# Attention in pairs of heads, in two row halves of TensorE, with fp32r parts in place of bf16 parts

## The reference

```python
q = (x @ Wqa @ Wqb).reshape(b, s, H, D)
kv = (x @ Wkva @ Wkvb).reshape(b, s, KVH, D, 2)
k, v = (kv[..., 0], kv[..., 1])
q = _rope(q)
k = _rope(k)
scores = jnp.einsum('bqhd,bkhd->bhqk', q, k) * scale
scores = jnp.where(causal[None, None], -jnp.inf, scores)
w = jax.nn.softmax(scores, axis=-1)
out = jnp.einsum('bhqk,bkhd->bqhd', w, v).reshape(b, s, E)
return out @ Wout + bout
```

## Time and profile before

| | us |
|---|---|
| median of 3 runs | 2591.58 |
| lowest, highest | 2581.57, 2600.53 |
| span of the profiled execution (first to last instruction) | 2609.7 |
| latents and routing | 0 to 199.4 |
| attention | 199.4 to 1299 |
| mixing | 1710 to 1859 |

### The profile page before, as it was taken

The page is one execution under the profiler, slowest core; times in us unless marked ns, Lnnn a source line. Parts: engine busy times, 40 slices in busy tenths (PEclk is TensorE's granted clock), DMA queues, the critical chain, the costliest instruction groups (busy, mean ns, idle before and its releaser), DMA issues. The chain is left out here.

```text
span 2609.7 us, 44812 instructions
## 1 busy us (share of the span) xinstructions
PE 2234.0 (86%) x12898; PEld 1283.6 (49%) x12898; DVE 1772.8 (68%) x3458; ACT 1179.7 (45%) x2552; POOL 772.4 (30%) x613
## 2 busy tenths in 40 slices
PE   5866889999999999999879999967578887798777
PEld 2322333333333333333369999946345544454446
DVE  3656667778887778777433333346498889988892
ACT  1222556666666666666644454411123333343332
POOL 3333333000000000000023333355156666566651
PEclk9756989999999999999989999976689898898897
DMA  7423333111111111111142223156400000000004
GB/s 280 130 70 104 96 104 103 57 56 58 58 58 56 58 56 58 57 57 57 30 146 94 97 81 109 49 159 196 145 1 16 17 17 0 16 16 16 9 0 141
DMA packets 140179, 191.32 MB, mean 73 GB/s; under 512 B 19256, under 2 KB 116416, under 8 KB 137920
## 3 DMA queue, kind: packets, MB, share of 16 engines
q1 hardware_dynamic: 111392, 139.92, 16.6%
q0 software_dynamic: 9120, 31.47, 3.7%
q10 hardware_dynamic: 19584, 18.88, 2.1%
HBM read 125.34 MB, written 60.29 MB: 71 GB/s over the span
## 5 line engine op out<-in xcount | busy, mean ns | idle before, releaser
L912 DVE TENSOR_REDUCE at_piece_max<-at_A 128x1 f32<-128x512 f32 (+3 forms) x1280 | 740.9, 605 | 249.3 <-PE at_A L809 205.9
L778 ACT ACTIVATE at_wt<-at_B 128x512 f32<-128x512 f32 (+3 forms) x1280 | 607.9, 537 | 339.1 <-PE at_B L833 211.9
L806 PE MATMUL at_A<-at_ka,at_qa 96*128 96x512 bf16 (+3 forms) x1280 | 459.1, 361 | 79.2 <-DMA at_ka<-k_parts 76.2
L830 PE MATMUL at_B<-at_qb,at_kb 99*128 99x512 bf16 (+3 forms) x1280 | 446.2, 353 | 1.7 <-ACT at_wt L778 0.6
L850 PE MATMUL at_O<-at_wt,at_v 128*32 128x512 f32 (+3 forms) x2496 | 339.2, 548 | 0.4 <-ACT at_wt L778 0.4
L806 PEld LDWEIGHTS at_A<-at_ka,at_qa 96*128 96x128 bf16 x1280 | 126.2, 99 | 432.7 <-DVE at_piece_max L912 245.8
L1176 POOL TENSOR_TENSOR s_down<-lw_down_full,s_down 128x256 fp32r<-128x256 f32 x10 | 7.3, 729 | 873.9 <-ACT lw_down_full L1168 873.9
L1353 PE MATMUL ex_H<-ex_xT,ex_w_in 128*128 128x256 f32 x1920 | 247.5, 285 | 3.2 <-DVE ex_xT L1460 3.2
L1353 PEld LDWEIGHTS ex_H<-ex_xT,ex_w_in 128*128 128x128 f32 x1920 | 236.6, 192 | 3.6 <-DVE ex_w_out L1465 3.6
L2051 POOL TENSOR_TENSOR l_sumy<-l_sumy,l_scaled 128x1024 f32<-128x1024 f32 x72 | 220.1, 3057 | 27.9 <-ACT l_scaled L2201 26.6
L2251 DVE TENSOR_TENSOR l_order<-l_order 128x1024 f32<-128x1024 f32 x112 | 221.2, 1975 | 1.9
(11 more groups left out here) (246 smaller groups left out, 3191.2 us busy)
## 6 DMA issues: line engine op xcount, KB each, us to landing
buf<-zeros POOLq DMA_DIRECT2D x10, 1024.0 KB, 20.6
ex_x<-buf SPq DMA_DIRECT2D x40, 256.0 KB, 2.7
expert_out<-ex_y ACTq DMA_DIRECT2D x40, 256.0 KB, 2.2
at_v<-v SPq DMA_DIRECT2D x32, 256.0 KB
ex_raw_in<-in_W_in SPq DMA_DIRECT2D x8, 1024.0 KB, 4.9
q_parts<-parts SPq DMA_DIRECT2D x16, 384.0 KB, 4.5
at_qa<-q_parts SPq DMA_DIRECT2D x32, 192.0 KB
at_ka<-k_parts SPq DMA_DIRECT2D x32, 192.0 KB
```

The source lines that it names most:

```text
L778: act.activation(wt[p % NE_][:, q0:CH], pB_of(p, u)[:, q0:CH], ACT.Exp, scale=D ** -0.5).then_inc(wt_ready, 1)
L806: ins = pe.matmul(pA[b][:, 0:w], qa[u][:, i * P:(i + 1) * P], ka[u][:, k0:k0 + w], start=True, stop=not diag)
L830: ins = pe.matmul(pB_of(p, u)[:, q0:CH], kb[u][:, kt * P:(kt + 1) * P], qb[u][:, j * CH + q0:(j + 1) * CH], start=True, stop=not diag)
L912: dve.tensor_reduce(piece_max[:, i, k0 // CH:k0 // CH + 1], pA[a_step(p) % NA][:, 0:w], AX.X, ALU.max).then_inc(a_used, 1)
```

## The change

In **latents** each of q and k is cut into two fp32r parts instead of three bf16 parts: one ScalarE cast and one GpSimd subtraction, whose result is the second part. The ScalarE casts L274 and the VectorE subtractions L401 are gone. The parts are stored as float32.

In **attention** a round is for a pair of heads that share their k and v. There are 16 rounds of 40 steps, and a step has two A pieces and two B pieces. The two heads stand in rows 0 to 63 and 64 to 127 of the operands, with three groups of 16 rows each (high by high, high by low, low by high) and, for B, two more rows for the maxima. Each pair of pieces waits once, for both buffers it needs; NA and NB stay 3, and NE_ is 16. The mask matmuls are gone: VectorE takes the diagonal maxima with a tensor_tensor_reduce that adds the mask from SBUF, and GpSimd zeroes the hidden half of each diagonal 128 x 128 block of wt by an affine_select. `values` handles four key tiles for both heads, eight matmuls in the four column groups (two groups a head, even and odd key tiles). The turn is four float32 matmuls with a 0/1 matrix of 64 columns that adds the two groups of each head, and ScalarE's `keep` copies result and sum to attn undivided. The loads are 12 two-dimensional DMAs of 16 rows for each of load_a and load_b, with one more for v, and four DMAs put rows of ones into kb before the first piece. GpSimd's indirect DMAs are tied to the rounds, two token tiles in each.

In **mixing** VectorE inverts the sums of all tiles at the start (512 in each partition), and GpSimd, behind its four gathers of a tile, writes at[u] as the product of attn and these; SyncE's copy is gone.

```diff
-PARTS = 3
+PARTS = 2
 VW = 32
 
-RUNS = ((0, 3), (3, 2), (5, 1))
-STACK = 6 * D
+Q_TERMS, K_TERMS = (0, 0, 1), (0, 1, 0)
+STACK = len(Q_TERMS) * D
+HP = 2
+BASE = P // HP
+HPAIRS = B * H // HP
...
-                pool.tensor_tensor(rest[k][0:rows], rot[k][0:rows], parts[k][0:rows, 0],
-                                   ALU.subtract).then_inc(rest_ready, 1)
+                pool.tensor_tensor(parts[k][0:rows, 1], rot[k][0:rows], parts[k][0:rows, 0].bitcast(F32),
+                                   ALU.subtract).then_inc(low_ready, 1)
...
-            def mid(c, k):
-                act.wait_ge(rest_ready, PAIRS * c + k + 1)
-                act.copy(parts[k][0:rows_of(k), 1], rest[k][0:rows_of(k)]).then_inc(mid_ready, 1)
...
-            def low(c, k):
-                dve.wait_ge(mid_ready, PAIRS * c + k + 1)
-                dve.tensor_tensor(parts[k][0:rows_of(k), 2], rest[k][0:rows_of(k)], parts[k][0:rows_of(k), 1],
-                                  ALU.subtract).then_inc(low_ready, 1)
...
-        NA, NB, NE_ = 3, 3, 8
+        NA, NB, NE_ = 3, 3, 16
         MR = PARTS
-        qa = [sb(f"qa{u}", [STACK, S], BF16) for u in range(2)]
-        ka = [sb(f"ka{u}", [STACK, S], BF16) for u in range(2)]
-        qb = [sb(f"qb{u}", [STACK + MR, S], BF16) for u in range(2)]
-        kb = [sb(f"kb{u}", [STACK + MR, S], BF16) for u in range(2)]
+        HALF_T = QT // 2
+        QKS = STACK + MR
+        qa = [sb(f"qa{u}", [P, S], F32R) for u in range(2)]
+        ka = [sb(f"ka{u}", [P, S], F32R) for u in range(2)]
+        qb = [sb(f"qb{u}", [P, S], F32R) for u in range(2)]
+        kb = [sb(f"kb{u}", [P, S], F32R) for u in range(2)]
...
+        def a_slot(p, h):
+            return HP * p + h + 2 * (p > M1_AT) + 2 * (p > M0_AT)
...
+        def stack(q, k, n):
+            for h in range(HP):
+                for r in range(len(Q_TERMS)):
+                    rows = slice(BASE * h + r * D, BASE * h + (r + 1) * D)
+                    cols = bass.ds(n // (H // HP) * S, S)
+                    yield q[rows, :].bitcast(F32), d["q_parts"][Q_TERMS[r], bass.ds(n % (H // HP) * HP * D + h * D, D), cols]
+                    yield k[rows, :].bitcast(F32), d["k_parts"][K_TERMS[r], bass.ds(n % (H // HP) // 2 * D, D), cols]
...
+            sp.wait_ge(ones_made, 1)
+            for u in range(2):
+                for h in range(HP):
+                    rows = kb[u][BASE * h + STACK:BASE * h + QKS, :]
+                    sp.dma_start(rows.rearrange("a (j n) -> a j n", n=CH).bitcast(F32),
+                                 ones[:].bitcast(F32).unsqueeze(1).to_broadcast([MR, NQ, CH])).then_inc(ones_in, 16)
...
+            def causal(n, p, h):
+
+                j, kt, q0 = Bp[p]
+                N = PER_B * n + HP * p + h
+                block_ = wt[(HP * p + h) % NE_][:, q0:q0 + P]
+                pool.wait_ge(wt_ready, N + 1)
+                pool.affine_select(block_, block_, [[1, P]], ALU.is_ge, 0.0, base=0,
+                                   channel_multiplier=-1).then_inc(hidden, 1)
+
+            fetch(0)
+            for n in range(HPAIRS):
+                for p in range(NPC):
+                    if p == END[1]:
+                        dispatch(n)
+                    if p == END[2] and n + 1 < HPAIRS:
+                        fetch(n + 1)
+                    if Bp[p][1] >= 4 * Bp[p][0]:
+                        for h in range(HP):
+                            causal(n, p, h)
...
+            def keep(n, j):
+                G = NQ * n + j
+                act.wait_ge(oT_made, G + 1)
+                dst = attn[:, bass.ds(n // (H // HP) * QT + j * TPC, TPC), bass.ds(n % (H // HP) * HP, HP), :]
+                src = pX_of(j).rearrange("p t (h n) -> p t h n", h=HP)[:, :, :, 0:D + 1]
+                act.copy(dst, src).then_inc(o_kept, 1)
...
+            def pieces_a(n, u, p):
                 i, k0, w = A[p]
-                N = PER_A * n + a_step(p)
-                b = a_step(p) % NA
                 if p == 0:
-                    pe.wait_ge(a_in[u], 6 * 16 * (n // 2 + 1))
+                    pe.wait_ge(a_in[u], LOADS * (n // 2 + 1))
+                wait(pe, a_used, PER_A * n + a_slot(p, HP - 1) - NA + 1)
+                for h in range(HP):
+                    rows = slice(BASE * h, BASE * h + STACK)
+                    pe.matmul(pA[a_slot(p, h) % NA][:, 0:w], qa[u][rows, i * P:(i + 1) * P], ka[u][rows, k0:k0 + w],
+                              start=True, stop=True).then_inc(a_made, 1)
...
+                wait(pe, wt_ready, PER_B * n + HP * p + 1 - NB + 1 + (u == 0 and p == 0))
+                for h in range(HP):
+                    rows = slice(BASE * h, BASE * h + QKS)
+                    pe.matmul(pB_of(p, h, u)[:, q0:CH], kb[u][rows, kt * P:(kt + 1) * P],
+                              qb[u][rows, j * CH + q0:(j + 1) * CH], start=True, stop=True).then_inc(b_made, 1)
...
             def values(n, u, p4):
+                pe.wait_ge(wt_ready, PER_B * n + HP * (p4 + VG))
+                wait(pe, hidden, PER_D * n + DIAG[p4 + VG])
+                j = Bp[p4][0]
+                if Bp[p4][1] == 0:
+                    wait(pe, o_kept, NQ * n + j - 1)
+                for p in range(p4, p4 + VG):
+                    kt, q0 = Bp[p][1:]
+                    for h in range(HP):
+                        rows = slice(VW * (2 * h + kt % 2), VW * (2 * h + kt % 2 + 1))
+                        late = kt == 1 and q0 > 0
+                        if late:
+                            pe.matmul(pO[j % 2][rows, 0:q0], blank[:], wt[(HP * p4 + h) % NE_][:, 0:q0],
+                                      start=True, stop=False)
+                        pe.matmul(pO[j % 2][rows, q0:CH], vs[u][:, kt // TPC, kt % TPC, :],
+                                  wt[(HP * p + h) % NE_][:, q0:CH], start=kt < 2 and not late,
+                                  stop=kt >= 4 * j + 2).then_inc(wt_used, 1)
...
-                    ins = pe.transpose(pX_of(j)[:, t, :], raw[j % 2][:, t * P:(t + 1) * P], ident[:])
+                    ins = pe.matmul(pX_of(j)[:, t, :], raw[j % 2][:, t * P:(t + 1) * P], summing[:], start=True, stop=True)
...
+                    p4 = p - LAG - VG + 1
+                    if p4 % VG == 0:
+                        if p4 >= 0:
+                            values(n, u, p4)
                         elif not first:
-                            values(n - 1, 1 - u, NPC - 3 - LAG + p)
+                            values(n - 1, 1 - u, NPC + p4)
...
+                        if p == (END[j] + LAG + VG - 1) % NPC and not (late and first):
+                            turn(n - late, j)
...
+                if diagonal:
+                    ins = dve.tensor_tensor_reduce(junk[(HP * i + h) % 4][:, 0:w], pA[slot % NA][:, 0:w], hide[:, CH - w:CH], 1.0, NEG,
+                                                   ALU.add, ALU.max, accum_out=top)
+                else:
+                    ins = dve.tensor_reduce(top, pA[slot % NA][:, 0:w], AX.X, ALU.max)
+                ins.then_inc(a_used, 1)
...
+                wait(pool, aT_made, t - 1)
+                both = bass.ds(2 * t, 2)
+                pool.tensor_tensor(at[u][:].rearrange("p w (h n) -> p w h n", n=D), s["attn"][:, both, :, 0:D],
+                                   over_sum[:, both].unsqueeze(3).to_broadcast([P, 2, H, D]),
+                                   ALU.mult).then_inc(at_ready, 1)
...
+            pool.wait_ge(sums_inverse, 1)
             rounds(pool, tile)
...
-                sp.dma_start(at[u][:], s["attn"][:, bass.ds(2 * t, 2), :]).then_inc(x_in[u], 16)
...
-                pe.wait_ge(x_in[u], 32 * (t // 2 + 1))
+                pe.wait_ge(at_ready, t + 1)
...
+            dve.reciprocal(over_sum[:], s["attn"][:, :, :, D]).then_inc(sums_inverse, 1)
```

More of the change, by code:

```diff
@@ L834, in piece_b @@
[L834 to L852 removed]
+                    pe.wait_ge(max_in[1], 32 * (n + 1))
@@ L1005, in layer1_weights @@
+            for n in range(HPAIRS):
+                round_(n, n + 1 < HPAIRS)
 def layer1_weights(nc, d, s):
```

412 lines of the change are left out of this document (169 added, 243 removed).

## The result

The change made the kernel slower: 2942.48 us (median of 4 runs, 2930.61 to 2956.77) against 2591.89 (4 runs), a ratio of 1.135 with a 95% interval of 1.131 to 1.140. The forecast was 2684, the range 2500 to 2790: the sign was right, the size was not, and the time lies outside the range. The profiled execution has a span of 2940.9 us against 2609.7, so 331 us are to be found.

A forecast was written before the change was run, and what follows sets the result against it. The prediction took PE and VectorE to hold each other through three buffers in attention. Attention +80.5 us, mixing +12 and latents 0 made +92.5, so 2684 us on the median, range 2500 to 2790.

The forecast's parts named there:

- The clock: Attention rounds: a quarter of the groups run at 1.2 GHz, adding 5.5 us a round, 64.2 to 69.7; called the weakest term.
- 86 with all: Attention: a round of two heads takes 86 us if all groups run at 1.2 GHz.
- What the clock rests on: PE in attention: fewer rows a us than now but longer bursts; clock near 0.88 on average.
- Rival 1: Attention: PE's clock stays at 2.4 GHz, rounds 64.2 us, +9 us, total 2601 us; chance 0.17.
- The round at 2.4 GHz: Attention, a pair of heads: VectorE work 46.0, idle 16.3, narrow pieces 0.9, correction 1.0, together 64.2 us.
- Rival 2: Attention: full values burst takes 1.0 us, rounds 56.4, total 2476 us; chance 0.29 including values between it and the high-clock rival.
- Rival 3: Attention: row halves do not overlap or selects are late, 2735 us and up; low clock throughout, 2930 us; chance 0.14.
- Latents: Latents stage: casts and third parts go, stored bytes rise by 4/3; 0 us (-5 to +6).
- Fill: Attention's start: first matmul at 225 us against 214.55 before, as twelve small loads replace a few wide ones.
- First pass: Attention's first pass, 80 pieces of A: 48 us, ending at 273 us.
- Last round: Attention's last round, only B: about 60 us, 61 with the clock.
- Mixing: Mixing: reciprocal 3.4 us with hand-overs +5, tiles 0.5 us further apart +7; in all +12 us (+5 to +22).

The follow-up runs named there:

- b1: Changed kernel with A and B matmuls reading all 64 rows of their half, zeros in the unused rows: 2887 us against the changed kernel's 2942, clock 0.79.
- e3: Kernel before without its mask matmuls, A and B reading 64 rows instead of 96 and 99: 2737 us, clock 0.84.
- b2: Kernel before with A matmuls reading 48 of their 96 rows: 2735 us, clock 1.00.
- e2: Kernel before without its 32 mask matmuls a head: 2606 us, clock 0.97.
- d2: Changed kernel with a wait for each single piece instead of one for each couple: 2887 us against the changed kernel's 2942, rounds 80.0 us.
- c1: Changed kernel with A and B reading all 64 rows of their half and each couple of A matmuls issued twice: 2956 us, clock 0.88.

## Why the prediction was wrong

- *The clock* is the step that failed: "I take a quarter of the groups at 1.2: 10 x 0.25 x 2.3 = 5.5" (the product is 5.75). The kind was right and named as the weakest term; both factors were low. At a mean of 0.70 PE spends 60% of the time, about half of the groups, at the low level. And a slow full group costs more than 2.3: the burst 3.64 instead of 1.92, four steps of 1.57 instead of 1.28, together 2.9, with turns of 1.97 instead of 1.10. 83.0 - 67 = 16 us a round instead of 5.5. What had been a bound "86 with all" would be about 100, by the same prices.
- *What the clock rests on*: I set fewer rows against longer bursts and took the middle. A head's matmuls of A and B read 48 and 50 rows where they read 96 and 99, at the same columns, and b1 and e3 show that the rows count; b2 shows that they do not decide alone. Why the clock of the changed kernel falls so often, 67 times where it fell 9 times, is not split further: with 64 rows (b1) it still fell 62 times. Masks, which I left out of the clock, don't matter (e2).
- *Rival 1*, clock at 2.4 GHz, came out false, and with it the reading that without a long pause the clock stays: at 835.4 us it fell with no pause over 0.6 us in the 7 us ahead. By the Trainium skill, "TensorE: Matmul & The Clock Gate", section "Why this matters for your kernels", gaps between matmuls make the clock fall. The trace agrees for the kernel before and e3, where each fall stands behind a pause of 1.3 to 4.9 us, and disagrees for the changed kernel.
- *The round at 2.4 GHz*: 67 instead of 64.2. The bursts were right (1.92 and 1.48 for 1.9 and 1.45), the turn 1.10 for 1.0. VectorE: reductions in a row start 0.61 us apart for 0.595, and the diagonal ones 0.62, so these cost nothing more, not 0.12, -3.8 us. What is left, over 6, is put down to idle time: a couple waits for two buffers, so a step takes 1.28 where two reductions take 1.22, and VectorE has less in store than the three pieces of the sum. Of that, d2 shows 3 us. The Trainium skill's rule that an accumulated output is a second instruction ("VectorE: DVE Perf Modes", section "Two Vector instructions with no wait between them") is seen, 83 ns, and it costs nothing.
- *Rival 2* fell with the burst: 1.92 us, over its point of 1.65.
- *Rival 3*: its first half did not come. The row halves overlap, the two matmuls of a couple start 3 ns apart and two couples take 0.56 us (c1). Its far end, the low clock throughout (2930 us), gave the measured time by too low a price: the clock was low 60% of the time, not all of it.
- *Latents*, put at 0 (-5 to +6): the attention began 27.3 us earlier. Part of it is scatter: it began at 186 to 199 us in four runs with the old latents and at 172 to 187 in thirteen with the new, 192 and 181 on the mean. Which of the dropped operations gives the 10 us was not tested.
- *Fill*: 41.5 us from the stage's start to the first matmul (172.1 to 213.6), against 15.2 before and 25.6 in the forecast (199.4 to 225). The seven variants without padding have 41.7 to 45.6. The profile puts the first matmul's wait to the rows of ones, the last of 43 transfers to be issued.
- *First pass*: 60.7 for 48. It is the couple's wait at the low clock: steps of 1.57 us, and with single waits 46.7 in all (d2). The three errors cancel, round 0 at 274 for 273: that is luck.
- *Last round*: 85.4 for 61. The forecast gave it 1 us for the clock; at a clock of 0.66 (0.59 in the window above) its groups take 7 to 8 us and 9 to 10 with a turn.
- The attention in sum: 15 x (83.0 - 69.7) = 200, last round 24, start 1: 225 us over the forecast's 1379.5, which is the measured 1604.7.
- *Mixing*: 20 for 12, in its range. The reciprocal took 3.35 for 3.4, the product 1.07 for 1.28; it stands ahead of tile 1's gathers too, and the tiles came 0.78 us further apart instead of 0.5.

## What to carry to other kernels

An edit that packs matmuls tighter takes work from TensorE; where another engine sets the pace, no time is won, and the clock can be lost, which every part that *was* bound by TensorE (here the float32 bursts) then pays at double length. Price such a change at both clock levels, and put the question which level holds to a cheap test: the old kernel with a lower operand (e3, 64 rows for the 48 and 50 to come) would have warned before anything was built. And a couple that waits for two of three buffers has turned a pipeline into a chain.
